# A gated cross-attention and feed-forward layer on one core: the sync engine issues a batch's transfers in another order

## The reference

```
x = x + tanh(g_xattn) * xattn(layernorm(x), ctx)      # 16 batches of 128 channels x 1024
x = x + tanh(g_ffn)   * ffn(layernorm(x))

xattn(x, cond):  q = Wq x + bq;  k = Wk cond + bk;  v = Wv cond + bv      # 8 heads of 16 channels
                 for each of 1024 positions t: softmax over the 16 k around t (padded with zeros),
                 times the 16 v around t;  then Wo ... + bo
ffn(x):          gate, up, down are 4-bit integers with a scale and a zero per group of 128 (1024 x 3584 x 2, 3584 x 1024)
                 silu(x gate) * (x up), times down
```

## Time and profile before

| | |
|---|---|
| median of 3 runs | 1617.93 us (1617.93, 1617.93, 1624.52) |
| the profiled execution's own time | 1623.17 us |
| its span | 1621.4 us |
| PE busy | 1534.6 us (95%) |
| DVE busy | 1454.5 us (90%) |
| POOL busy | 1262.2 us (78%) |
| ACT busy | 1057.2 us (65%) |

### The profile page before, as it was taken

How to read it: one execution, slowest core, us unless ns; L and a number is a source line. 1 busy time by engine, 2 the same in 40 slices (tenths; PEclk the granted TensorE clock), 3 DMA queues, 4 the chain that set the end, 5 groups by cost and what they waited for, 6 DMA issues and landing times.

```text
span 1621.4 us, 38499 instructions
## 1 busy us (share of the span) xinstructions
PE 1534.6 (95%) x15590; PEld 789.4 (49%) x15590; DVE 1454.5 (90%) x1425; ACT 1057.2 (65%) x1207; POOL 1262.2 (78%) x948
## 2 busy tenths in 40 slices
PE   6888898988799999999999999999999999999996
PEld 4565566665444444444444444444444444444444
DVE  4688788887798999999999999999999999999997
ACT  3677777877566666666666666666666666666652
POOL 3677677778455988888888888888888888888865
PEclk7899999999899999999999999999999999999999
DMA  4676766775353767666667676666666676666569
GB/s 126 171 155 140 172 145 148 173 159 138 118 143 98 152 154 155 152 151 152 147 153 156 156 155 151 149 153 152 152 155 156 144 156 156 153 152 151 116 182 324
DMA packets 192267, 250.16 MB, mean 154 GB/s; under 512 B 14446, under 2 KB 138030, under 8 KB 192074
## 3 DMA queue, kind: packets, MB, share of 16 engines
q1 hardware_dynamic: 167994, 164.26, 36.8%
q0 software_dynamic: 22752, 82.85, 29.1%
q10 hardware_dynamic: 1344, 0.59, 0.2%
HBM read 113.92 MB, written 16.78 MB: 81 GB/s over the span
## 4 chain that ended last, share of the span: by engine, by line
PE 86%; ACT 5%; issue 4%; POOL 2%; DVE 1%; DMA 1%; SPq 1%; ACTq 0%; DVEq 0%; POOLq 0%
PE bank L1193 69%; PE bank L1111 3%; PE bank L1100 2%; ACT pT L684 2%; PE bank L1066 2%; PE bank L1131 2%; PE bank L1073 2%; PE bank L1062 2%; PE bank L1058 1%; ACT vn_hl L662 1%; POOL oacc L628 1%; PE bank L1078 1%; PE bank L1090 1%; ACT pr L679 1%; ACT xn L692 1%
## 5 line engine op out<-in xcount | busy, mean ns | idle before, releaser
L988 DVE SCALAR_TENSOR_TENSOR acc<-bank,scale,acc 128x1024 f32<-128x1024 f32 x784 | 969.5, 1279 | 51.7 <-PE bank L1193 14.9
L1193 PE MATMUL bank<-xT,w_int 128*128 128x512 f16 x3584 | 847.8, 379 | 6.3 <-DVE xT L940 2.0
L628 POOL TENSOR_TENSOR oacc<-oacc,d_part 128x1024 f32<-128x1024 f32 x219 | 536.3, 2454 | 54.5 <-ACT d_part L832 49.0
L1193 PEld LDWEIGHTS bank<-xT,w_int 128*128 128x128 f16 x3584 | 350.3, 98 | 431.4 <-DVE xT L940 3.3
L832 ACT ACTIVATE d_part<-bank,scale 128x1024 f32<-128x1024 f32 x219 | 244.1, 1115 | 200.8 <-PE bank L1193 196.9
L1193 PE MATMUL bank<-h_hi,d_int 128*128 128x512 f16 x896 | 339.6, 379 | 2.1 <-ACT d_part L832 1.8
L1193 PE MATMUL bank<-h_lo,d_int 128*128 128x512 f16 x896 | 339.6, 379 | 0.0
L832 ACT ACTIVATE d_more<-bank,scale 128x1024 f32<-128x1024 f32 x158 | 176.2, 1115 | 154.4 <-PE bank L1193 154.4
L630 POOL DMA_DIRECT2D oacc<-d_more x158 | 149.9, 949 | 114.0 <-ACT d_more L832 107.8
L564 POOL TENSOR_TENSOR raw_z<-raw_w,raw_z 128x512 int32<-128x512 int32 x168 | 225.6, 1343 | 16.5 <-DMA raw_z<-in_L_ffn_gate_z_dram 8.3
L684 ACT ACTIVATE pT<-bank 96x1024 f16<-96x1024 f16 x128 | 130.2, 1017 | 38.3 <-PE bank L1111 37.9
(11 more groups left out here) (85 smaller groups left out, 1438.5 us busy)
## 6 DMA issues: line engine op xcount, KB each, us to landing
oacc<-d_more POOLq DMA_DIRECT2D x158, 512.0 KB, 5.0
raw_w<-in_L_ffn_gate_w_dram SPq DMA_DIRECT2D x56, 256.0 KB, 3.4
raw_z<-in_L_ffn_gate_z_dram SPq DMA_DIRECT2D x56, 256.0 KB, 4.2
raw_w<-in_L_ffn_up_w_dram SPq DMA_DIRECT2D x56, 256.0 KB, 3.4
raw_z<-in_L_ffn_up_z_dram SPq DMA_DIRECT2D x56, 256.0 KB, 4.0
raw_w<-in_L_ffn_down_w_dram SPq DMA_DIRECT2D x56, 256.0 KB, 3.1
raw_z<-in_L_ffn_down_z_dram SPq DMA_DIRECT2D x56, 256.0 KB, 3.7
vt<-vn_hl SPq DMA_DIRECT2D x64, 198.0 KB
```

The source lines that it names most:

```text
L628: nc.gpsimd.tensor_tensor(into, into, d_part[:, (n - 1) % 2, :], ALU.add).then_inc(d_added, 1)
L988: nc.vector.scalar_tensor_tensor(out=into, in0=pair[u % 4][:, :, :].rearrange("p h r -> p (h r)"), scalar=scale[:, par, i, m, k:k + 1], in ...
L1193: last = nc.tensor.matmul(dst[:, h, :], weights, rows_of(h, part), start=(part == 0), stop=(part == 1))
```

## The change

In the loop over batches SP's five steps come in another order, and v's two copies are taken apart: first k's moves, then the row's store, then v's first copy, the context's load, v's second copy, and x's load. No transfer is added, removed or resized; each keeps its waits (the second copy repeats those of the first).

```diff
-            def place_v(b):
+            def place_v(b, copies=(0, 1)):
...
-                for d in (0, KW):
+                for copy in copies:
+                    d = KW * copy
...
             for b in range(B):
                 if b == B - 1:
                     first_weights(range(2))
+                if b + 1 < B:
+                    move_k(b + 1)
                 if b >= 2:
                     keep_row(b - 2)
                 if b == B - 1:
                     first_weights(range(2, N_CAST))
                 if b + 1 < B:
-                    move_k(b + 1)
+                    place_v(b + 1, (0,))
                 if b + 2 < B:
                     load_ctx(b + 2)
                 if b + 1 < B:
-                    place_v(b + 1)
+                    place_v(b + 1, (1,))
                 if b + 2 < B:
                     load_x(b + 2)
```

## The result

The changed kernel takes 1610.87 us (median of 15 runs, 1605.12 to 1616.94); the kernel before, run beside it, 1625.44 us (15 runs, 1615.25 to 1631.31). The ratio is 0.9918 [0.9898, 0.9938]: 0.8% faster. That is outside the predicted range of 1613 to 1632 us, and on the other side of "no change" than the forecast's +4.7 us.

A forecast was written before the change was run, and what follows sets the result against it. It took engines waiting a little for one another at many places as the bound, with SP's order nearly free. Terms 2.9 + 0.5 + 1.3 = 4.7 us gave 1622.6 us on the 1617.93 us median; range 1613 to 1632 us.

The forecast's parts named there:

- the one on *x: Full batches: x lands 1.3 us later behind the store, so DVE waits in six batches, 2.9 us in sum.
- SP's order costs next to nothing now: Full batches: SP is idle part of each batch, so making a transfer earlier brings little; one may become late.
- My last sign of being wrong: In the changed kernel's profile: PE's "issue" stalls change by more than all the other predicted effects.
- The faster rival: Full batches: parting x and store frees x by 1.1 us and removes two PE stalls, 7 to 8 us; chance 0.08.
- The queue-bound rival: Full batches: context delayed 3 us or more, PE stands 1.3 us in some ten batches, 13 us; chance 0.22.
- the room I had given it: Full batches: the later context lands at 172.2, 1.7 us before PE's projection of k, costing 0 us.
- The absorbed rival: Full batches: PE and DVE make up for x's lateness, 0 to 2 us remain, 1619 us; chance 0.20.
- k's moves: Start of SP's batch order: SP waits for k before and after, so nothing changes, 0 us.
- the store's landing: Load of x into the store's buffer: comes about 10 us after issue against 6.8 us to landing, 0 us.
- The start: Batch 0: PE stands 3.6 us for the later context, mostly hidden by its own stall; 0.5 us, between 0 and 3.6.
- The end: Batches 14 and 15: store ahead of the last v delays POOL's first weights by 1.3 us (0.4 to 1.7).
- The rule of the Trainium skill: DMA queue: the first eight engines are full, so nothing of the store is absorbed; sum between 4.7 and 10.6 us.

The follow-up runs named there:

- e1: Against the kernel before, only the store moved, to behind k's moves; the context stays ahead of both of v's copies: 1650.3 us, ratio 1.0167.
- e2: Against the kernel before, only the context's load moved, to between v's two copies; the store stays ahead of k's moves: ratio 0.9997.
- e5: Against the kernel before, only the store moved, into the middle of k's moves: ratio 0.9955.
- e10: Against the kernel before, the store moved into the middle of k's moves and the context's load between v's copies: 1611.0 us, ratio 0.9889.
- e12: Against e10, x's load moved ahead of the last three transfers of v's second copy: 1621.12 us, ratio 0.9952.

## Why the prediction was wrong

**The step that failed** is the one on *x*: "the store is now in the queue ahead of it: 1.3 us later at landing". That term, 2.9 of the 4.7 us, was to be waits of DVE. Measured, *x* lands in 5.5 us, not 7.2, and DVE waits 0.8 us in sum (0.7 before), not 3. I priced the store as 512 KB that delay all behind them, down to a load issued 10 us later. But it lands in 3.1 us (6.5 before), so it is gone before the second copy of v begins. I also left out the other side: the store used to fly *with* *x*, and that companion is now gone.

**The premise that failed** is larger: "SP's order costs next to nothing now, and the change can bring little". I counted a transfer as costing only what someone waits for at its landing. PE's code comes over the same DMA engines, and its lateness stands in no row that names a transfer. It stood in the earlier trace rows as "2.35 issue" and the earlier trace rows as "3.04 issue", and I used both as given. Over the same matmuls PE's "issue" waits fell from 28.5 to 22.3 us, which is most of the 8.8 us gained there. My last sign of being wrong, "issue" stalls that change by more than all of the sum's 4.7 us, came true.

**The faster rival** (0.08, 1610 us) named half the mechanism and nearly the time: *x* and the store fly together, and the stall at 125.99 comes out of that flight. I held the fuller queue under v against it. What I had not seen is that the context beside v's first copy costs the same kind of stall at another place, and that moving the store alone would have made the rival's opposite come true. By e1 and e2 both moves were needed. And its condition as I gave it, parting the two, is not enough by itself (e1 1.0167).

**The queue-bound rival** (0.22, 1632 us) did come true, for a kernel that wasn't the change: e1, where the store stands ahead of context and v, is 1.67% slower, though by PE's code and not by the context: in e1 PE never waits for the context in full batches. In the change the order puts the context behind v's first copy, and it arrives in time. Its median of 6.0 us to landing lies inside the forecast's 4.8 to 7.5. In the batch shown it took longer, by the DMA issues from 162.4 to 162.6 us:

```profile
ct<-in_ctx_dram SPq DMA_DIRECT2D x1, 512.0 KB, 7.2
```

So it lands at 162.48 + 7.2 = 169.7 us, 1.7 us ahead of PE's projection in the chain of waits, which is the room I had given it:

```profile
171.35 1.77 PE bank L1065 x4
```

**The absorbed rival** (0.20, 1619 us) had the right reading of DVE but no gain in it.

**The smaller terms.** *k's moves* at 0 and *the store's landing* awaited by nobody: right, no row of SP's waits at L376 names the store. *The start*: right in size. PE stands 3.9 us for the context, forecast 3.6, and its own stall in that place is gone, so that DVE's moments come at 59.45 in place of 59.26: 0.2 us, forecast 0.5. PE's timeline:

```profile
53.62 3.75 PE L1065 MATMUL bank<-ct,wk 128*128 128x512 f32 x4 [3.89 <-DMA ct<-in_ctx_dram]
```

*The end*: wrong. POOL's wait for the first weights was to grow from 0.75 to about 2 us and is 0.70; SP's wait for v's last copy ahead of them, which was to be longer, is 3.0 us where it was 2.9. *The spread*: my sum started from one execution and the median of three runs, 1617.93, where 15 runs give 1625.44. The change's 1610.87 is 14.6 us below the later median and 7.1 below the earlier. The earlier alone would have left it within my bound of 8.1 us for no change; the ratio above, from 15 runs of each, does not.

**The rule of the Trainium skill** ("DMA: Bandwidth & Descriptors", "Queues, rings and completion order"), by which nothing of the store would be absorbed and the sum would be 4.7 us or more, gave the wrong sign as well. That a full queue holds all behind it back does show in e1 (*x* at 9.2 us), where the store and the context stand together. The same section says that a DMA engine takes turns between its queues packet by packet. By that a code packet would wait for about one packet of q1; the trace has none of q8 for 8.7 us under a full q1, and the next starts 6.0 us after PE has passed the place ahead. That is no contradiction as long as the time of the request is unknown, but it does not bear the rule out either.

**What stays open.** Why the code is late (held in the engines, or asked for late) isn't shown; the times above speak for a request made when PE passes the place ahead, and then held. The waits are of one profile each. All "issue" over the same matmuls goes well with the time of that stretch (the two last columns of the table: correlation 0.95 over the fifteen profiles, 1.55 us of time for 1 us of "issue"); the three columns of single places rank the kernels only roughly. The ratio goes with it a little less closely (0.91), as a profile is one execution: e5's took 1627.86 us, 9 us over that kernel's median. Why more than 1 us goes for each us of stall is shown in part, by the granted clock in e1. In e2 the gain at the turning is lost at the mixing (8.8 to 14.7), where *x* and the store still fly together but with a late context ahead of them; that this is the cause was argued from e10, in which the mixing falls to 2.0 us, and not tested alone. Why the code is late at one place and not at the next is theory E's part, and e12 shows that it is incomplete. The stalls at v's projection come in every order, 4.4 to 13.6 us. They stand at the same row of places and so are code too; where it was read (before, the change and e1) their packets follow the one before by 3.4 to 5.4 us only, so they look like code used up fast, and no run aimed at them.

## What to carry to other kernels

An engine that stops at "issue" in the middle of equal instructions, in a program that is written out at length, may be out of code. Two things tell: a packet of the instruction queue ends shortly before each such stall does, and the stalls of different versions of the kernel stand at the same instructions, evenly spaced. Then look for the large transfers that fill the DMA engines just ahead. Their order has a price even when nobody waits for their landings; here it fell on PE. Look at the granted clock behind long stalls too: in e1 PE's busy time grew by 12.1 us beside 15.1 us of stalls. Test the parts of such a reordering singly and together, since they interact: here +1.7% and 0 made -0.8%.

## What the runs showed of the hardware

- PE's code arrives in packets of 16 KB over a queue of its own (q8), one for about 125 matmuls and their weight loads, on the same DMA engines. With q1 at 87 to 92% there were stretches of 6.7 and 8.7 us without one, and stalls of PE up to 4.06 us, ended 1.2 to 1.9 us after the next packet. All 305 stalls of 0.5 us or more stood at 59 places, 125 to 127 matmuls or twice that apart.
- In e1 TensorE's granted clock fell from 1.00 to 0.50 after each of ten stalls of 2.0 to 4.1 us, and the same matmuls kept PE busy for 264.9 us, where it was 252.9 before.
- The same 512 KB on the same queue land in 3.1 us (the store behind k's small moves), 4.1 us (*x* between v's copies), 5.9 us (*x* with the store behind it) or 9.2 us (*x* in e1). What is issued *behind* a load seems to matter too: the change puts the store's 512 KB ahead of *x* instead of behind it, and *x* is 0.4 us quicker; but the store is then also issued 10 us earlier, and no run parts the two.
